# GpSimd multiplies the value rows of thirteen blocks in the last batch of a graph attention layer

## What is computed

```python
Vh = (x @ Wv + bv).reshape(N, NUM_HEADS, HEAD_DIM)
alpha = jax.nn.leaky_relu(s[src] + s[dst], NEG_SLOPE)
m = jax.ops.segment_max(alpha, dst, num_segments=N)
e = jnp.exp(alpha - m[dst])
denom = jax.ops.segment_sum(e, dst, num_segments=N)
a = e / denom[dst]
msg = Vh[src] * a[:, :, None]
attn = jax.ops.segment_sum(msg, dst, num_segments=N).reshape(N, D_MODEL)
h = attn @ Wo + bo
```

## Time and profile before

| | |
|---|---|
| median of three runs | 4308.77 us (4302.22 to 4315.38) |
| the profiled execution | 4308.08 us, of which 4306.3 us are the span |
| PE busy | 3277.9 us, 76% |
| DVE busy | 2147.4 us, 50% |
| POOL busy | 3020.7 us, 70%, nearly all of it gathers |
| line 1835, multiply, 196 times | 238.9 us, 1219 ns each |
| line 1840, 0/1 matrices, 488 times | 224.0 us, 482 ns each |

### The profile page before, as it was taken

The page is one execution under the profiler, slowest core; times in us unless marked ns, Lnnn a source line. Parts: engine busy times, 40 slices in busy tenths (PEclk is TensorE's granted clock), DMA queues, the critical chain, the costliest instruction groups (busy, mean ns, idle before and its releaser), DMA issues. The chain is left out here.

```text
span 4306.3 us, 75198 instructions
## 1 busy us (share of the span) xinstructions
PE 3277.9 (76%) x13728; PEld 2372.7 (55%) x13729; DVE 2147.4 (50%) x6078; ACT 487.8 (11%) x1111; POOL 3020.7 (70%) x3154
## 2 busy tenths in 40 slices
PE   3777777777777777777788778887777777776798
PEld 2565555555555555555566555565655555555544
DVE  6434333333333333333455555545577777777733
ACT  4000000000000000000011101101011111111122
POOL 5777777777777777777777777776777777777200
PEclk9888889898888888888999999999888889898999
DMA  6444434435344344344444444445655555554411
GB/s 202 121 136 124 124 106 124 125 105 143 105 125 125 105 125 124 106 125 127 130 140 136 142 136 136 142 135 155 162 147 157 148 159 147 157 146 138 127 60 60
DMA packets 284796, 563.69 MB, mean 131 GB/s; under 512 B 104638, under 2 KB 176133, under 8 KB 279691
## 3 DMA queue, kind: packets, MB, share of 16 engines
q0 software_dynamic: 150528, 414.45, 34.0%
q10 hardware_dynamic: 70180, 89.46, 6.3%
q1 hardware_dynamic: 63974, 58.59, 4.4%
HBM read 487.19 MB, written 73.45 MB: 130 GB/s over the span
## 5 line engine op out<-in xcount | busy, mean ns | idle before, releaser
L763 POOL DMA_INDIRECT arena<-h_table,idx_v x2292 | 2174.3, 949 | 726.3 <-issue 694.0
L895 PE MATMUL banks<-arena 128*128 x5856 | 1544.9, 420 | 617.9 <-SPq L790 506.0
L895 PEld LDWEIGHTS banks<-arena 128*128 128x128 f32 x5856 | 1171.5, 208 | 957.2 <-issue 774.4
L842 DVE TENSOR_SCALAR arena<-iota_t,dst_e 128x128 f32<-128x128 f32 x2928 | 846.8, 310 | 821.7 <-PE banks L895 575.9
L1278 POOL DMA_INDIRECT arena<-vs_table,idx_v x764 | 765.0, 1001 | 232.8 <-issue 228.8
L1496 PE MATMUL banks<-arena 128*128 x1952 | 518.8, 416 | 52.8 <-DVE arena L1840 52.6
L1496 PEld LDWEIGHTS banks<-arena 128*128 128x128 f32 x1952 | 366.5, 199 | 192.5 <-issue 120.4
L916 PE MATMUL banks<-arena,lhs 128*128 128x256 f32 x1176 | 339.6, 439 | 5.0 <-ACT lhs L1016 0.2
L948 DVE TENSOR_SCALAR small<-banks 128x1 f32<-128x1 f32 x147 | 23.2, 158 | 638.7 <-PE banks L897 638.7
L1016 ACT ACTIVATE lhs<-banks 128x512 f32<-128x512 f32 x147 | 87.8, 597 | 2073.7 <-PE banks L907 2073.5
L916 PEld LDWEIGHTS banks<-arena,lhs 128*128 128x128 f32 x1176 | 240.5, 215 | 100.8 <-ACT lhs L1016 64.8
(11 more groups left out here) (263 smaller groups left out, 2468.4 us busy)
## 6 DMA issues: line engine op xcount, KB each, us to landing
arena<-h_table,idx_v POOLq DMA_INDIRECT x2292
arena<-dst_dram SPq DMA_DIRECT2D x14, 1792.0 KB
arena<-vs_table,idx_v POOLq DMA_INDIRECT x764
h_table<-arena ACTq DMA_DIRECT2D x11, 1024.0 KB, 7.4
h_early<-arena ACTq DMA_DIRECT2D x10, 1024.0 KB
vs_table<-arena ACTq DMA_DIRECT2D x49, 132.0 KB
x_dram<-arena ACTq DMA_DIRECT2D x49, 128.0 KB
hln_dram<-arena ACTq DMA_DIRECT2D x49, 128.0 KB
```

The lines of the kernel that those rows point to most:

```text
L763: pool.indirect_dma_start(ring[:, s * BJ + j, 0:width], None, table, bass.IndirectOffsetOnAxis(idx_v[:, half, n * BJ + j:n * BJ + j + 1], ...
L842: dve.tensor_scalar(onehot[:, j, :], iota_t[:], dst_e[:, bass.ds(b * BJ + j, 1)], None, ALU.is_equal).then_inc(W["onehot_made"], 1)
L895: pe.matmul(agg[:, 0:D + 1], onehot[:, j, :], ring[:, (b % SLOTS) * BJ + j, 0:D + 1], start=False, stop=False).then_inc(W["onehot_used"], 1)
```

## The change

In the last batch VectorE multiplies only the first block. The other thirteen are multiplied by GpSimd, behind its last gather. GpSimd reads the weights from the ring's columns `D` to `VS`, since they are there as well as in PSUM. It waits once for these (`edge_placed`) and once for VectorE's first block, so that `rows_ready` counts on in order, and then issues thirteen multiplies with no wait between them.

```diff
@@ attend_gpsimd @@
             first_and_rest(pool, KS // 2, rounds)
+            pool.wait_ge(G["edge_placed"], KS)
+            pool.wait_ge(G["rows_ready"], (KS - 1) * BB + 1)
+            for s in range(1, BB):
+                rows = batch_slots(KS - 1)[:, s * BJ:(s + 1) * BJ, :]
+                v = rows[:, :, 0:D].rearrange("p j (h c) -> p j h c", h=HEADS)
+                w = rows[:, :, D:VS].rearrange("p j (h o) -> p j h o", o=1)
+                pool.tensor_tensor(v, v, w.broadcast_to([P, BJ, HEADS, C]), ALU.mult).then_inc(G["rows_ready"], 1)
@@ attend_vector, weigh, pairs @@
                         with dve.Fori(b0 + 1, b1 + 1) as b:
-                            weighted(b, b - (k - k % 2) * BB, b - k * BB)
+                            if k + 1 < KS:
+                                weighted(b, b - (k - k % 2) * BB, b - k * BB)
                             src_onehots(t, b)
```

## The result

The changed kernel is slower: 4316.26 us median of 11 runs (4313.75 to 4326.74) against 4305.36 of 11 for the kernel before, a ratio of 1.0025 with a 95% interval of 1.0017 to 1.0033. That is +10.9 us. The forecast was +17.5 (4326 us, range 4303 to 4335).

The account below looks back on a forecast made before the run. TensorE paces the feed-forward; in the last batch VectorE is only just slower than TensorE. Block 184's matrices 19.6 us late, 3.8 back from stalls, 1.7 added for clock: +17.5 us, 4326 us, range 4303 to 4335.

Parts of the forecast that it names:

- The bound: Feed-forward runs at TensorE's pace, untouched; only the last batch's end can move, and everything behind moves by the same amount.
- The gain of 4.4 us: Last batch: 13 multiplies taken off VectorE remove TensorE's 7 stalls for the 0/1 matrices, 4.4 us.
- GpSimd's rows in time: Last batch: GpSimd's multiplied blocks come before TensorE needs them, unless a multiply takes over 3.3 us.
- The meeting, a full turn each: VectorE's instructions with two SBUF inputs and GpSimd's multiplies alternate; block 184's matrices 19.6 us late; chance 0.47.
- no meeting: Rival: last-batch VectorE instructions run beside GpSimd's multiplies unheld, gaining 4.4 us, 4304.4 us; chance 0.22.
- VectorE first: Rival: VectorE waits only when arriving mid-multiply, 5 us lost against 4.4 gained, 4309 us; chance 0.15.
- GpSimd first: Rival: 13 multiplies run unbroken, VectorE gets in only at 4068.7; +21 us, 4330 us; chance 0.13.
- the stretched gather: Evidence for engines waiting on each other: beside line 1762's scan a GpSimd gather takes 1.92 us, others 0.95.
- The sum: Last batch: 19.6 us late, 3.8 back from stalls, 1.7 added for TensorE's clock: +17.5 us.
- The multiply: Each GpSimd multiply of 1024 elements in the last batch takes 2.2 us, bounds 0.94 and 2.6.
- VectorE's turn back: VectorE's held matrices and attention instructions between GpSimd's multiplies add 4 x 0.48 + 3 x 0.17 + 3 x 0.42 = 3.7 us.
- The clock's part: TensorE's clock drops behind the new stall of some 17 us, as after the softmax; 1.7 us added.

Follow-up runs that it names:

- e2: Changed kernel with PSUM operands, so no last-batch VectorE instruction has two SBUF inputs: ratio to the kernel before 0.9988, again 0.9993; stretch 262.6 and 262.3 us against 267.4.
- e1: Changed kernel, but the last batch's 0/1 matrices read the edges' ends from PSUM: stretch 273.2 us against 267.4 before; ratio to the kernel before 1.0007.
- e3: Kernel before, plus 13 GpSimd multiplies on spare memory whose results nobody reads: stretch 280.7 us against 267.4; ratio to the kernel before 1.0023.
- e5: Kernel before, plus 13 GpSimd copies of 1024 elements from spare to spare memory: stretch 273.3 us against 267.4, one run.
- e6: Changed kernel, but GpSimd multiplies only seven blocks, 189 to 195: stretch 276.0 us against 267.4 before; ratio to the kernel before 1.0025.
- e7: Changed kernel with only the attention's small sums and product in PSUM: stretch 271.8 us against 267.4 before; ratio to the kernel before 1.0001.

## Why the prediction was right

**The bound.** Right. Outside the batch nothing moved: from the end of the batch's last matmul (4088.03 + 2.10 in the earlier trace rows) to the end of the span it is 216.2 us before, and within 0.1 us of that in every other profile.

**The gain of 4.4 us.** Right in size, and hidden in the result. e2 shows it on its own: 4.4 us from the second tile on, in both of its profiles.

**GpSimd's rows in time.** Right. TensorE waited for none; all of its waits in the batch are on the matrices.

**The meeting, a full turn each.** Right as a mechanism, and it had been the step that no row priced. VectorE's instructions with two SBUF inputs were stretched to about a multiply's length, each in a turn; the three rivals (no meeting, VectorE first, GpSimd first) are excluded by the timeline above, e1 and e3: the attention's small instructions stand right behind one another and are held one by one, and VectorE gets in after each multiply. What was off is the return: the prediction let the next multiply wait for all of VectorE's instruction, and it hardly waits (below). Taking the full turn from the stretched gather in the earlier trace rows was partly luck. In that row GpSimd waits for VectorE, here it is mostly the other way; a gather beside line 1840 isn't stretched; and no run shows what a gather has in common with a multiply. The Trainium skill (SBUF — State Buffer, SBUF: two separate sides) states this rule, with two SBUF inputs on VectorE's side and a read of SBUF on GpSimd's; e1 to e5 agree with each half of it. By the Trainium skill (the same section) whichever comes first keeps the ports until its instruction is done, and the 1.83 us for 8 elements agree.

**The sum.** Too large by some 7 us, in sizes and not in kind. The 0.25% measured is slower beyond its own interval, but under the 0.3% at which I had set the line for slower, so the likelier of my calls (0.53) missed its own line; 4316.26 us also lies under the 4320 to 4332 that I gave as the forecast's own range. That it lies in 4303 to 4335 says little, as this range took in the case without a meeting too. Three terms of the sum:

- *The multiply*: 2.2 us taken, 1.87 measured (24.35 / 13 in e2, where nothing meets it). It was inside the bounds 0.94 and 2.6; two streams read in turn would be 1.8. Over the 12 multiplies that lie ahead of block 184's matrices this is 4.0 us. The Trainium skill's figure (GPSIMD Engine Reference, 3.1 Elementwise) gave an estimate of 2.25, and the measurement is 17% under it.
- *VectorE's turn back*: 3.7 us taken for ten instructions between the multiplies. The thirteen multiplies last 25.87 us with meetings and 24.35 without, so GpSimd lost only 1.5 us in all, of which 1.4 ahead of block 184's matrices. A multiply that follows a held matrix takes 2.09 us, one that follows an instruction on 8 elements 1.91, as long as in e2 (rows below). This is 2.3 us of the sum.
- *One turn too many*: line 1823 ran right behind 1821 in the same turn, at 0.41 us, so twelve multiplies and not thirteen lay ahead of block 184's matrices: 2.2 us.

Two of GpSimd's multiplies in the changed kernel:

```profile
4056.75 2.09 POOL L1307 TENSOR_TENSOR arena<-arena 128x1024 f32<-128x1024 f32 x1
...
4062.90 1.91 POOL L1307 TENSOR_TENSOR arena<-arena 128x1024 f32<-128x1024 f32 x1
```

Together 8.5 us: block 184's first matmuls come 25.65 us after the batch's first multiply and came 14.62 after it before, so 11.0 us late where the sum had 19.6, 8.6 more. Behind them 3.8 us less 1.7 for the clock were to come back; 11.0 - 9.8 = 1.2 did. The clock's part was under-sized: 40 matmuls in 12.72 us against 9.94 are 2.8 us, with the second matrix of block 184 still held among them.

## What to carry to other kernels

Moving work to an idle engine adds its footprint on what it shares with the others. Before giving GpSimd an operation that reads SBUF, list VectorE's instructions beside it that have two SBUF inputs: each, however small, may take as long as one of GpSimd's, and a chain of small dependent ones is the worst case (0.17 to 1.83 us; five of the seven in the attention are held, and together the seven take 8 us more). Putting one operand of each into PSUM took the whole loss away here; having GpSimd do half as much work in a worse place did not. And count the clock behind a new stall of TensorE as a term of its own: it was 2.2 to 3 us in e6, e7 and the changed kernel.

## What I had not expected of the hardware

The hold is one-sided. VectorE's instructions grew by up to 1.7 us, GpSimd's thirteen by 1.5 us in total. And it stands inside the busy time of the one that waits, so neither the waits nor the idle times name it; what shows it is the mean length of one instruction form against its own length elsewhere in the same trace.
